# Residual rows kept in DRAM: experts' outputs added by accumulating scatters

## The chip, the cores and the metric

One core of a Trainium2 chip. The metric is the device time of one execution in microseconds (us). TensorE multiplies matrices, VectorE, ScalarE and GpSimd compute elementwise, SyncE issues transfers; all of a core's transfers run on its 16 DMA engines. SBUF is the memory on the chip, with 128 partitions, PSUM takes TensorE's results, and DRAM (HBM) is the memory outside.

## The reference

Four sublayers change x, which has 32 x 256 tokens of 128 floats:

```
x = x + attention_a(layernorm(x))       # 16 heads, product of two score matrices, causal
x = x + experts(layernorm(x))           # layer 0
x = x + attention_b(layernorm(x))       # features, softmax over 256 tokens, causal
x = x + experts(layernorm(x))           # layer 1, same weights

experts(x):
  feat   = x as 8192 rows of 128
  norm   = layer_norm(feat, g, b)
  scores = norm @ centroids.T                       # 8 experts
  for each expert in turn: the 1024 best tokens that no earlier expert took
  routed = feat[chosen tokens]                      # 8 x 1024 x 128
  h      = gelu(layer_norm(routed, g, b) @ w1 + b1) @ w2 + b2    # 128 -> 512 -> 128
  out    = routed + h, put back at the tokens' places
```

Each token is chosen by exactly one expert. The experts get a normalised x, so x + experts(layernorm(x)) is x + layernorm(x) + h: the first two terms are x times a factor plus a shift for each token, and h is the experts' own row.

## The kernel before

x stays in SBUF for the whole kernel, as `k["x"]`: 64 tiles of 128 tokens (token 128 n + p lies in partition p of tile n), 4 MB. The kernel is a row of phases, each with its own blocks for the engines. `phase` (line 74) calls the body, has GpSimd clear the phase's semaphores and then holds all engines at a barrier, so no phase overlaps the next. `build` lists them: load_x, statistics, attention_a, normalise_for_experts, experts, add_rows, statistics, attention_b, normalise_for_experts, experts, add_rows. Two DRAM tensors of 8192 rows lie between phases: `norm_rows` holds the normalised rows that the experts gather, `ffn_rows` takes the experts' outputs.

`experts` (line 798) works in turns (`plan`, line 913): in turn e the engines search the tokens of expert e (VectorE compares, TensorE counts), list those of expert e - 1 as row numbers, and compute expert e - 2. What each engine does in it:

- SyncE (lines 937 to 956) loads the weights of expert e, and from expert 2 on waits for the copy of expert e - 2's output first (`y_copied`), since two sets of weight buffers take turns. After expert 7 it has nothing left.
- ScalarE starts with a pass over the 64 tiles of x in place (line 1263): x times a factor plus a shift, which is x + layernorm(x). Each tile raises `x_done`. Then it copies and activates for the experts; line 1296 copies an expert's output from PSUM into the buffer `yb`, in two halves, and waits until the scatters of the expert two before have left that buffer.
- GpSimd gathers (line 1321) and scatters (line 1328): eight indirect DMAs each for an expert, each of 128 rows of 512 bytes, with the row numbers from the list `index`. In turn e it scatters expert e - 3, half by half, and then gathers expert e - 1; in the last turn it scatters expert 7 too. All of these go through GpSimd's own DMA queue. At the end it waits until all scatters have landed (line 1346).
- TensorE turns the gathered rows (line 1150), multiplies with w1 (line 1159) and w2 (line 1169).

The scatters of before write h alone into `ffn_rows`. `add_rows` (line 1349) then reads `ffn_rows` back in the order of the tokens, in eight groups of eight tiles (0.5 MB) through four buffers, and VectorE adds each group to x (line 1382). For layer 0 VectorE then measures mean and variance of the group's eight tiles (`bn_stats`, line 1386), which the next statistics phase needs. For layer 1 ScalarE stores each group to the output instead (line 1374).

The functions that the change touches:

Of the kernel before, what the change touches and what calls it, by code (L numbers as in the profile page):

```python
# [13 lines left out]
F32 = mybir.dt.float32  # L14
# [4 lines left out]
ALU = mybir.AluOpType  # L19
# [3 lines left out]
P = 128  # L23
D = 128
B, T = 32, 256
TOKENS = B * T
TILES = TOKENS // P
# [23 lines left out]
def wait_apart(eng, semaphore, value, passed):  # L51


    eng.wait_ge(semaphore, value)
    eng.sem_inc(passed, 1)
# [14 lines left out]
def phase(nc, body, *args):  # L70

    used = []

    def sem(name):
        used.append(nc.alloc_semaphore(name))
        return used[-1]

    body(nc, sem, *args)
    nc.clear_and_free_semaphores(used)
    nc.all_engine_barrier()  # L80


def build(nc, d):
    with ExitStack() as whole:
        def keep(name, shape, dt=F32):
            return whole.enter_context(nc.sbuf_tensor(name, shape, dt))

        k = {
            "x": keep("x", [P, TILES, D]),
            "ident": keep("ident", [P, P]),  # L90
            "rstd": keep("rstd", [P, TILES]),
            "shift": keep("shift", [P, TILES]),
            "halves": keep("halves", [P, TILES, 6]),
            "high_key": keep("high_key", [P, E, TILES], U16),
            "low_key": keep("low_key", [P, E, TILES], U16),
            "rstd_1": keep("rstd_1", [P, TILES]),
            "gain": keep("gain", [P, 1]),
            "bias": keep("bias", [P, 1]),
            "cent": keep("cent", [P, 32]),
            "digits": keep("digits", [P, PASSES, CANDS], U32),  # L100
            "weight": keep("weight", [P, PASSES]),
            "before": keep("before", [P, P], BF16),
            "lanes": keep("lanes", [P, P, TILES // CHUNKS], BF16),
            "place": keep("place", [P, 2 * SLOTS, TILES], BF16),
            "eighth": keep("eighth", [P, 2 * SLOTS, TILES], BF16),
            "w_all": keep("kept_w_all", [P, FEAT + D]),
            "w_shell": keep("kept_w_shell", [SHELL, D]),
            "omega_t": keep("kept_omega_t", [SHELL, RFF]),
            "b_shell": keep("kept_b_shell", [SHELL, P]),
            "b_all": keep("kept_b_all", [P, FEAT + D]),  # L110
            "b_rff": keep("kept_b_rff", [P, RFF]),
            "temp": keep("kept_temp", [P, 1]),
            "decay": keep("kept_decay", [P, T]),
            "c_mag": keep("kept_c_mag", [P, NM]),
            "w_comb": keep("kept_w_comb", [P, 3, P]),
            "w_out": keep("kept_w_out", [P, D]),
            "b_out": keep("kept_b_out", [P, D]),
            "bar": keep("kept_bar", [P, P], BF16),
            "ident_b": keep("kept_ident_b", [P, P], BF16),
            "b_consts": nc.alloc_semaphore("attention_b_consts"),  # L120
            "consts": nc.alloc_semaphore("expert_consts"),
            "norm_consts": nc.alloc_semaphore("norm_consts"),
        }
        k["scores"] = keep("scores", [P, E, TILES])
        norm_rows = nc.dram_tensor("norm_rows", (TOKENS, D), F32, kind="Internal").ap()
        ffn_rows = nc.dram_tensor("ffn_rows", (TOKENS, D), F32, kind="Internal").ap()
        phase(nc, load_x, d, k)
        phase(nc, statistics, k, "a")
        phase(nc, attention_a, d, k)
        phase(nc, normalise_for_experts, d, k, norm_rows, 0)  # L130
        phase(nc, experts, d, k, norm_rows, ffn_rows, 0)
        phase(nc, add_rows, k, ffn_rows, None, 0)
        phase(nc, statistics, k, "b")
        phase(nc, attention_b, d, k)
        phase(nc, normalise_for_experts, d, k, norm_rows, 1)
        phase(nc, experts, d, k, norm_rows, ffn_rows, 1)
        phase(nc, add_rows, k, ffn_rows, d["out"], 1)
        nc.clear_and_free_semaphores([k["consts"], k["norm_consts"], k["b_consts"]])
        nc.all_engine_barrier()

# [657 lines left out]
def experts(nc, sem, d, k, norm_rows, ffn_rows, layer):  # L798
# [4 lines left out]
    tag = f"e{layer}"  # L803
    per = TILES // CHUNKS
# [4 lines left out]
    with ExitStack() as ctx:  # L809
# [60 lines left out]
        rows = [sb(f"rows{i}", [P, SLOTS, D]) for i in range(2)]  # L870
# [3 lines left out]
        yb = [sb(f"yb{i}", [P, SLOTS, D]) for i in range(2)]  # L874
# [34 lines left out]
        y_copied = sem(f"y_copied_{tag}")  # L909
        scattered = [sem(f"scattered{i}_{tag}") for i in range(2)]  # L910
        wait_passed = sem(f"passed_{tag}")

        def plan(eng, turn):

# [22 lines left out]
        with nc.Block() as block:  # L937
            @block.sync
            def _(sp):
                def turn(e, par, half):  # L940
                    if isinstance(e, int) and e >= E:
                        return
                    at = bass.ds(e, 1) if not isinstance(e, int) else slice(e, e + 1)
                    w1_src = d["L0_ffn_w1"][at, :, :].rearrange("a p f -> (a p) f")
                    w2_src = d["L0_ffn_w2"][at, :, :].rearrange("a (p c) n -> (a p) c n", c=FC)
                    b1_src = d["L0_ffn_b1"][at, :].rearrange("a (p c) -> (a p) c", c=FC)
                    b2_src = d["L0_ffn_b2"][at, :].broadcast_to([P, D])

                    if not isinstance(e, int) or e > 1:
                        sp.wait_ge(y_copied, 2 * e - 2)  # L950
                    sp.dma_start(w1[par][:], w1_src).then_inc(wl[par], 16)
                    sp.dma_start(w2[par][:], w2_src).then_inc(wl[par], 16)
                    sp.dma_start(b1[par][:], b1_src).then_inc(wl[par], 16)
                    sp.dma_start(b2[par][:], b2_src).then_inc(wl[par], 16)

                plan(sp, turn)

# [354 lines left out]
            def _(pool):  # L1312
# [10 lines left out]

                def scatter(c, par, half, h):
                    part = slice(h * SLOTS // 2, (h + 1) * SLOTS // 2)
                    wait_apart(pool, y_copied, 2 * c + h + 1, wait_passed)
                    for j in range(part.start, part.stop):
                        pool.indirect_dma_start(ffn_rows, bass.IndirectOffsetOnAxis(ap=list_of(c, par)[:, j:j + 1], axis=0),  # L1328
                                                yb[par][:, j, :], None).then_inc(scattered[par], 16)

                def turn(e, par, half):
                    _, lists, compute = does(e)
# [13 lines left out]
                    pool.wait_ge(scattered[par], 16 * SLOTS * (E // 2))  # L1346


def add_rows(nc, sem, k, rows_dram, out, layer):

    tag = f"r{layer}"
    steps = 8
    per = TILES // steps
    with ExitStack() as ctx:
        buf = [ctx.enter_context(nc.sbuf_tensor(f"buf{i}_{tag}", [P, per, D], F32)) for i in range(4)]
        loaded = [sem(f"rows_loaded{i}_{tag}") for i in range(4)]
        added = sem(f"rows_added_{tag}")
        measured = sem(f"rows_measured_{tag}")
        stored = sem(f"out_stored_{tag}")
        rows = rows_dram.rearrange("(n p) d -> p n d", p=P)  # L1360
        out_v = out.rearrange("b (t p) d -> p (b t) d", p=P) if out is not None else None
        with nc.Block() as block:
            @block.sync
            def _(sp):
                for g in range(steps):
                    if g >= 4:
                        sp.wait_ge(added, g - 3)
                    sp.dma_start(buf[g % 4][:], rows[:, g * per:(g + 1) * per, :]).then_inc(loaded[g % 4], 16)  # L1368
            if out is not None:
                @block.scalar  # L1370
                def _(act):
                    for g in range(steps):
                        act.wait_ge(added, g + 1)
                        act.dma_start(out_v[:, g * per:(g + 1) * per, :], k["x"][:, g * per:(g + 1) * per, :]).then_inc(stored, 16)
                    act.wait_ge(stored, 16 * steps)

            @block.vector
            def _(dve):
                for g in range(steps):
                    dve.wait_ge(loaded[g % 4], 16 * (g // 4) + 16)  # L1380
                    part = k["x"][:, g * per:(g + 1) * per, :]
                    dve.tensor_tensor(part, part, buf[g % 4][:], ALU.add).then_inc(added, 1)  # L1382
                    if out is None:
                        dve.wait_ge(added, g + 1)
                        for n in range(g * per, (g + 1) * per):
                            dve.bn_stats(k["halves"][:, n, :], k["x"][:, n, :]).then_inc(measured, 1)


def attention_b(nc, sem, d, k):
# [567 lines left out]
```

## Time and profile before

| | us |
|---|---|
| median of 3 runs (lowest to highest) | 1505.43 (1504.72 to 1506.91) |
| profiled execution, its own time | 1510.9 |
| its span, first to last instruction | 1509.1 |
| experts, layer 0, from SyncE's first load to GpSimd's last scatter | 591.2 to 891.5 |
| add_rows, layer 0, from the first reload to the last statistics | 896.5 to 923.0 |
| experts, layer 1, end of the last scatter | 1475.2 |
| add_rows, layer 1, from the first reload to the span's end | 1480.3 to 1509.1 |

A line of the timeline gives the start from the span's beginning, the duration, the engine, the line of the kernel, the operation with its output and inputs, how many instructions are merged in it, and in brackets how long the engine had stood idle and what ended that. PE is TensorE, PEld its weight load, DVE VectorE, ACT ScalarE, POOL GpSimd, SP SyncE; SPq is SyncE issuing DMAs, and its duration is that of the issuing, not of the transfer.

### The profile page before, as it was taken

How to read it: one execution, taken by the hardware profiler on the slowest of the kernel's cores; microseconds unless marked ns; L12 is line 12 of the kernel's file. 1: busy time of each engine (PE TensorE's matmuls, PEld its weight loads, DVE VectorE, ACT ScalarE, POOL GpSimd, SP SyncE). 2: the span in 40 equal slices, each digit the busy share in tenths (PEclk: the TensorE clock that was granted, in tenths of full speed). 3: DMA queues.
4: the chain of work that ended last, by engine and by line, in shares of the span. 5: the costliest groups of instructions: out<-in, count | busy, mean ns of one | idle time of the engine just before them, and what ended most of it. 6: DMA issues, size and time to landing. Idle time of an engine off the chain costs nothing. (4 is left out here: it accounts for less than half of the span.)

```text
span 1509.1 us, 33959 instructions
## 1 busy us (share of the span) xinstructions
PE 1156.4 (77%) x11356; PEld 742.7 (49%) x11356; DVE 921.9 (61%) x2822; ACT 701.2 (46%) x1485; POOL 731.0 (48%) x712
## 2 busy tenths in 40 slices
PE   0799999999999966478887942769996358888790
PEld 0244444444444433156655732659993136666570
DVE  4477767777777757887764016845557786766102
ACT  0477676767767637322222314655554602322240
POOL 0478878787878840045456430045550024545540
PEclk9999999999999987579998875979998559999895
DMA  6000000000000004011121132000003101111118
GB/s 167 4 2 0 0 0 0 0 0 0 0 0 0 1 6 140 2 28 50 45 67 55 50 85 53 0 1 0 0 0 112 33 15 46 50 52 49 56 50 229
DMA packets 67979, 54.64 MB, mean 36 GB/s; under 512 B 12864, under 2 KB 57280, under 8 KB 67904
## 3 DMA queue, kind: packets, MB, share of 16 engines
q1 hardware_dynamic: 51392, 32.70, 7.8%
q0 software_dynamic: 8192, 16.79, 3.8%
q10 hardware_dynamic: 8320, 4.19, 0.9%
q8 instruction: 42, 0.69, 0.2%
q14 instruction: 33, 0.27, 0.1%
HBM read 32.69 MB, written 20.97 MB: 36 GB/s over the span
## 5 line engine op out<-in xcount | busy, mean ns | idle before, releaser
L353 POOL TENSOR_TENSOR patt_aa<-patt_aa,causal_aa 128x512 f32<-128x512 f32 x256 | 319.4, 1273 | 73.6 <-DVE patt_aa L477 71.8
L477 DVE TENSOR_TENSOR patt_aa<-p_second_aa,first_aa 128x512 f32<-128x512 f32 x384 | 247.5, 686 | 136.2 <-ACT first_aa L410 132.5
L410 ACT ACTIVATE first_aa<-p_first_aa 128x512 f32<-128x512 f32 x384 | 208.7, 597 | 139.0 <-PE p_first_aa L568 135.1
L1321 POOL DMA_INDIRECT rows_e<-norm_rows,index_e x128 | 123.8, 967 | 269.5 <-DVE index_e L1037 210.2
L568 PE MATMUL p_second_aa<-q_t_aa,k_t_aa 32*128 32x512 f32 x768 | 235.4, 642 | 0.0
L568 PE MATMUL p_first_aa<-q_t_aa,k_t_aa 32*128 32x512 f32 x768 | 217.4, 642 | 15.7 <-ACT first_aa L410 15.4
L1328 POOL DMA_INDIRECT ffn_rows<-yb_e,index_e x128 | 128.1, 1001 | 163.5 <-ACT yb_e L1296 129.9
L1237 PE MATMUL p_cnt_e<-reach_e,ones_e 128*128 128x240 bf16 x448 | 88.0, 330 | 82.4 <-DVE reach_e L1083 76.6
L1159 PE MATMUL p_h_e<-rows_t_e,w_e 128*128 128x512 f32 x256 | 146.1, 694 | 0.2
L1288 ACT ACTIVATE hid_e<-p_h_e,b_e 128x512 f32<-128x512 f32 x128 | 88.0, 687 | 125.1 <-PE p_h_e L1159 102.9
L587 PEld LDWEIGHTS p_z_aa<-patt_aa,v_aa 128*32 128x32 f32 x3072 | 72.4, 109 | 147.5 <-issue 78.9
L1169 PE MATMUL p_y_e<-w_e,hid_e 128*128 128x128 f32 x1024 | 144.1, 286 | 0.3 <-issue 0.2
L1169 PEld LDWEIGHTS p_y_e<-w_e,hid_e 128*128 128x128 f32 x1024 | 133.0, 203 | 0.8 <-issue 0.6
L587 PE MATMUL p_z_aa<-patt_aa,v_aa 128*32 128x128 f32 x3072 | 124.1, 279 | 2.8 <-POOL patt_aa L353 2.8
L568 PEld LDWEIGHTS p_first_aa<-q_t_aa,k_t_aa 32*128 32x128 f32 x768 | 57.7, 183 | 97.9 <-ACT first_aa L410 88.7
L1382 DVE TENSOR_TENSOR x<-x,buf_r 128x1024 f32<-128x1024 f32 x16 | 19.5, 1218 | 141.1 <-DMA buf_r<-ffn_rows 141.1
L1278 ACT ACTIVATE rows_t_e<-p_t_e,bias,gain 128x512 f32<-128x512 f32 x32 | 25.0, 781 | 171.9 <-PE p_t_e L1150 171.9
L347 POOL TENSOR_TENSOR roped_aa<-straight_aa,crossed_aa 128x512 f32<-128x512 f32 x64 | 81.3, 1271 | 44.7 <-DVE crossed_aa L467 44.7
L1237 PEld LDWEIGHTS p_cnt_e<-reach_e,ones_e 128*128 128x128 bf16 x448 | 39.8, 110 | 128.1 <-DVE reach_e L1083 94.3
L1159 PEld LDWEIGHTS p_h_e<-rows_t_e,w_e 128*128 128x128 f32 x256 | 71.5, 317 | 36.5 <-issue 33.0
L397 ACT ACTIVATE q_t_aa<-p_turn_aa,own_aa 128x512 f32<-128x512 f32 x128 | 81.6, 698 | 2.5 <-PE p_turn_aa L551 2.5
L1096 DVE TENSOR_REDUCE count_e<-p_cnt_e 128x15 f32<-128x240 f32 x112 | 45.4, 406 | 52.3 <-PE p_cnt_e L1237 28.5
(242 smaller groups left out, 2158.2 us busy)
## 6 DMA issues: line engine op xcount, KB each, us to landing
norm_rows<-norm_n SPq DMA_DIRECT2D x32, 256.0 KB, 2.4
w_e<-L_ffn_w SPq DMA_DIRECT2D x32, 256.0 KB
buf_r<-ffn_rows SPq DMA_DIRECT2D x16, 512.0 KB, 6.2
out<-x ACTq DMA_DIRECT2D x8, 512.0 KB, 8.5
rows_e<-norm_rows,index_e POOLq DMA_INDIRECT x128
ffn_rows<-yb_e,index_e POOLq DMA_INDIRECT x128
b_e<-L_ffn_b SPq DMA_DIRECT2D x16, 64.0 KB
lanes<-c_lanes SPq DMA_DIRECT2D x1, 256.0 KB, 2.8
```

Source lines behind the costliest of these rows:

```text
L353: pool.tensor_tensor(patt[n % LAG][:, b, :, :], patt[n % LAG][:, b, :, :], causal[:, None, :].broadcast_to([P, 4, P]), ALU.mult).then_inc( ...
L397: act.activation(q_t[par][:, :, j, :], p_turn[:, :].rearrange("p (h q) -> p h q", h=HALVES), ACT.Identity, scale=own[:, j:j + 1]).then_inc ...
L410: act.activation(first[n % 2][:, b, :], p_first[b][:], ACT.Identity).then_inc(first_copied, 1)
L477: dve.tensor_tensor(patt[n % LAG][:, b, :, :].rearrange("p h q -> p (h q)"), p_second[(2 * n + b) % ROOMS][:], first[n % 2][:, b, :], ALU. ...
L568: pe.matmul(out[:], k_t[par][rows, half, keys * P:(keys + 1) * P], q_t[par][rows, half, :, queries * P:(queries + 1) * P], start=True, sto ...
L587: mm = pe.matmul(p_z[32 * c:32 * c + 32, queries * P:(queries + 1) * P], v[par][:, keys, 32 * h:32 * h + 32], patt[n % LAG][:, b, c, :], s ...
L1159: pe.matmul(p_h[m % 2][:], w1[par][:, f:F:FC], rows_t[:, h * 512:(h + 1) * 512], start=True, stop=True).then_inc(up_done, 1)
L1169: mm = pe.matmul(p_y[t // 4][:, (t % 4) * D:(t % 4 + 1) * D], hid[:, f, t * P:(t + 1) * P], w2[par][:, f, :], start=False, stop=(f == FC - 1))
L1237: mm = pe.matmul(p_cnt[:, 0:SPAN * CANDS], ones[:], reach[:, q // 2, :, (q % 2) * SPAN:(q % 2 + 1) * SPAN], start=(q == 0), stop=(q == TIL ...
L1288: act.activation(hid[:, f, h * 512:(h + 1) * 512], p_h[m % 2][:], ACT.Gelu_apprx_tanh, bias=b1[par][:, f:f + 1]).then_inc(gelu_done, 1)
L1321: pool.indirect_dma_start(rows[lpar][:, j, :], None, norm_rows, bass.IndirectOffsetOnAxis(ap=list_of(l, lpar)[:, j:j + 1], axis=0)).then_i ...
L1328: pool.indirect_dma_start(ffn_rows, bass.IndirectOffsetOnAxis(ap=list_of(c, par)[:, j:j + 1], axis=0), yb[par][:, j, :], None).then_inc(sc ...
```

## The change

The experts' phase now also stores x to DRAM. After the weights of expert 1 SyncE issues eight stores of eight tiles each, each as soon as ScalarE has finished those tiles; they go to the tensor that the experts' rows are scattered into. The scatters add to what lies there (`compute_op=ALU.add`) instead of overwriting it, and the first of them waits until all eight stores have landed. For layer 1 that tensor is the kernel's output itself, and nothing follows. For layer 0 it is `ffn_rows`, and the phase behind loads it straight over x in eight loads without buffers, with the statistics of each group and without an add.

```
-        phase(nc, add_rows, k, ffn_rows, None, 0)
+        phase(nc, load_rows, k, ffn_rows)
...
-        phase(nc, experts, d, k, norm_rows, ffn_rows, 1)
-        phase(nc, add_rows, k, ffn_rows, d["out"], 1)
+        phase(nc, experts, d, k, norm_rows, d["out"].rearrange("b t d -> (b t) d"), 1)
...
+        x_stored = sem(f"x_stored_{tag}")
+        parts = 8
...
+                def store_x():
+                    for q in range(parts):
+                        tiles = slice(q * TILES // parts, (q + 1) * TILES // parts)
+                        sp.wait_ge(x_done, (q + 1) * TILES // parts)
+                        sp.dma_start(ffn_rows.rearrange("(n p) d -> p n d", p=P)[:, tiles, :], k["x"][:, tiles, :]).then_inc(x_stored, 16)
...
                     sp.dma_start(b2[par][:], b2_src).then_inc(wl[par], 16)
+                    if e == 1:
+                        store_x()
...
                 def scatter(c, par, half, h):
                     part = slice(h * SLOTS // 2, (h + 1) * SLOTS // 2)
+                    if c == 0 and h == 0:
+                        pool.wait_ge(x_stored, 16 * parts)
                     wait_apart(pool, y_copied, 2 * c + h + 1, wait_passed)
                     for j in range(part.start, part.stop):
                         pool.indirect_dma_start(ffn_rows, bass.IndirectOffsetOnAxis(ap=list_of(c, par)[:, j:j + 1], axis=0),
-                                                yb[par][:, j, :], None).then_inc(scattered[par], 16)
+                                                yb[par][:, j, :], None,
+                                                compute_op=ALU.add).then_inc(scattered[par], 16)
...
+def load_rows(nc, sem, k, rows_dram):
+
     steps = 8
     per = TILES // steps
...
+    loaded = [sem(f"rows_loaded{g}") for g in range(steps)]
+    measured = sem("rows_measured")
+    rows = rows_dram.rearrange("(n p) d -> p n d", p=P)
+    with nc.Block() as block:
+        @block.sync
+        def _(sp):
+            for g in range(steps):
+                sp.dma_start(k["x"][:, g * per:(g + 1) * per, :], rows[:, g * per:(g + 1) * per, :]).then_inc(loaded[g], 16)
+
+        @block.vector
+        def _(dve):
+            for g in range(steps):
+                dve.wait_ge(loaded[g], 16)
+                for n in range(g * per, (g + 1) * per):
+                    dve.bn_stats(k["halves"][:, n, :], k["x"][:, n, :]).then_inc(measured, 1)
```

## Rows read from the trace of the kernel before

**Rows 1.** The page: the span, and its 40 slices of TensorE.
```profile
span 1509.1 us, 33959 instructions
...
PE   0799999999999966478887942769996358888790
```

**Rows 2.** The chain that ended last: by line, and its last piece.
```profile
by line: DMA buf_r<-ffn_rows 1.2%; DVE x L1382 0.2%; SPq L1368 0.1%; issue 0.0%
...
1501.40 1.23 DVE x L1382
```

**Rows 3.** Timeline of the span's end, layer 1's last scatters and reload.
```profile
1465.37 0.96 POOL L1328 DMA_INDIRECT ffn_rows<-yb_e,index_e  x1 [6.50 <-ACT yb_e L1296]
...
1474.27 0.97 POOL L1328 DMA_INDIRECT ffn_rows<-yb_e,index_e  x1 [0.30 <-issue]
1480.28 12.23 SPq L1368 DMA_DIRECT2D buf_r<-ffn_rows  x8
1484.51 1.23 DVE L1382 TENSOR_TENSOR x<-x,buf_r 128x1024 f32<-128x1024 f32 x1 [66.49 <-DMA buf_r<-ffn_rows]
```

**Rows 4.** By stretch: PE, PEld, DVE, ACT, POOL busy, clock, DMA share, GB/s.
```profile
1492.00:1496.00 4.00, 0.00 (x0) 0.00 (x0) 1.89 (x2) 0.00 (x0) 0.00 (x0) 0.50 1.15 347
```

**Rows 5.** Timeline of add_rows after layer 0, and the next phase's first instruction.
```profile
896.51 14.00 SPq L1368 DMA_DIRECT2D buf_r<-ffn_rows  x8
900.49 1.23 DVE L1382 TENSOR_TENSOR x<-x,buf_r 128x1024 f32<-128x1024 f32 x1 [66.35 <-DMA buf_r<-ffn_rows]
901.75 1.64 DVE L1386 BATCH_NORM_STATS2 halves<-x 128x6 f32<-128x128 f32 x8
...
921.36 1.64 DVE L1386 BATCH_NORM_STATS2 halves<-x 128x6 f32<-128x128 f32 x8
923.78 0.06 DVE L212 MEMSET eps_b<- 128x1 f32 x1 [0.78 <-PEq L80]
```

**Rows 6.** GpSimd's DMA queue, 640 to 892: packets, MB, share of 16 engines.
```profile
q0 software_dynamic: 4064, 8.33, 11.3%
```

**Rows 7.** By stretch: the reload of layer 0, and the features behind it.
```profile
898.00:900.00 2.00, 0.00 (x0) 0.00 (x0) 0.00 (x0) 0.00 (x0) 0.00 (x0) 0.50 0.98 290
...
908.00:910.00 2.00, 0.00 (x0) 0.00 (x0) 2.00 (x7) 0.00 (x0) 0.00 (x0) 0.50 0.92 243
...
936.00:950.00 14.00, 13.59 (x77) 12.47 (x75) 9.64 (x28) 13.87 (x35) 0.00 (x0) 0.94 0.00 0
```

**Rows 8.** ScalarE's pass over x (timeline); SyncE's waits: total, times, longest.
```profile
591.24 24.73 ACT L1263 ACTIVATE x<-x,shift,rstd 128x128 f32<-128x128 f32 x64 [4.18 <-PEq L80]
...
SPq L951 <- ACT yb_e L1296: 213.1, 5, 93.4
```

**Rows 9.** Scatters' and gathers' lines; queue and 40 slices, 1465 to 1476.5; a 16 KB load.
```profile
L1328 POOL DMA_INDIRECT ffn_rows<-yb_e,index_e x128: 963/969/1435, 677.0 to 1474.3; - x128
...
L1321 POOL DMA_INDIRECT rows_e<-norm_rows,index_e x128: 940/944/1170, 638.5 to 1427.5; - x128
...
DMA  0000005100060006000140006000320006000510
...
q0 software_dynamic: 256, 0.52, 13.4%
...
rope_aa<-c_rope SPq DMA_DIRECT2D x1, 16.0 KB, 2.0
```

**Rows 10.** Timeline: gathers, TensorE's turning of their rows, a scatter.
```profile
704.78 0.94 POOL L1321 DMA_INDIRECT rows_e<-norm_rows,index_e  x1 [0.30 <-issue]
...
715.54 0.60 PE L1150 MATMUL p_t_e<-ident,rows_e 128*128 128x128 f32 x4
...
1413.73 0.94 POOL L1321 DMA_INDIRECT rows_e<-norm_rows,index_e  x1 [0.30 <-issue]
...
1431.17 1.00 POOL L1328 DMA_INDIRECT ffn_rows<-yb_e,index_e  x1 [2.69 <-ACT yb_e L1296]
1431.31 0.60 PE L1150 MATMUL p_t_e<-ident,rows_e 128*128 128x128 f32 x4
```

More of the change, by code:

```diff
@@ L1346, in _ @@
                     pool.wait_ge(scattered[par], 16 * SLOTS * (E // 2))
-def add_rows(nc, sem, k, rows_dram, out, layer):
-    tag = f"r{layer}"
+def load_rows(nc, sem, k, rows_dram):
     steps = 8
     per = TILES // steps
[L1354 to L1386, printed above, removed]
```

## The prediction

> **What bounds the kernel now.** I read the page first, then the chain that ended last, then the timeline around both places where the experts' stage hands over, then the scatters and gathers inside it.
>
> The page's slices show TensorE at 9 tenths for much of the span of 1509.1 us, but at nothing in the last slice of 37.7 us [rows 1], and the chain of waits is nothing but the last stage: 1.2% of the span in the reload, 0.2% in the adds, down to the add at 1501.40 [rows 2]. So the kernel is a row of stages, and two of them are pure data movement in which TensorE stands still. The second one: GpSimd's last scatter ends at 1475.24, SyncE's first reload is issued at 1480.28, VectorE's first add starts at 1484.51, and the span ends at 1509.1 [rows 2, 3]. The reader is to see that eight adds of 1.23 us are spread over 18 us: they wait for loads, and from 1492 the loads share the engines with the output's stores at 347 GB/s in total [rows 4]. The first one, after layer 0, has the same head (first reload 896.51, first add 900.49), but here VectorE is the bound: one add of 1.23 us and eight statistics of 1.64 us together for each of eight groups, without a gap that a load causes, until 923.00 [rows 5].
>
> Inside layer 0's experts' stage GpSimd's queue, with 64 gathers and 64 scatters per layer, takes 11.3% of 16 engines [rows 6]: transfers are not what its turns wait for. At the stage's end the last matmuls, the last copy and the last scatters follow each other.
>
> **The change part by part.** All sums are first against the profiled execution: span 1509.1, its own time 1510.9, so 1.8 us lie around the span. The median shown is 1505.43, 5.5 us below that execution. I carry the difference over unchanged.
>
> 1. Last stage dropped. The span's part from the first reload to the end is 1509.1 - 1480.28 = 28.8 us [rows 1, 3]. What remains is the final clearing of three semaphores and one barrier. A hand-over between two phases costs VectorE 0.78 us from its last instruction to its next [rows 5], with a block's end in it, so the rest is between 0 and 0.78; I take 0.4. Gain 28.4 us. The 5.04 us between the last scatter's end and 1480.28 (landing, GpSimd's block end, barrier) stay.
>
> 2. Layer 0's stage becomes a plain load. No buffer is waited for, so the loads run at their own rate. The trace shows 290 GB/s from 898 to 900, where four groups are on the way [rows 7]: 0.524 MB / 0.29 = 1.81 us a group. First group ready at 900.49 as now, the eighth at 900.49 + 7 x 1.81 = 913.2, its eight statistics 1.64: 914.8. The first seven groups' statistics (1.64 each) hide under the loads by 0.17 us each. Before: 923.0. Gain 8.2 us. Bounds: 9.8 us if loads were no limit (8 adds of 1.23); 5 us if they ran at 243 GB/s, as in 908 to 910 (2.16 a group, end 917.3, gain 5.7). What is late next is the load, not VectorE.
>
> 3. x stored from SyncE: eight DMAs of 0.5 MB per layer, behind the weights of experts 0 and 1. ScalarE writes the 64 tiles from 591.24 to 615.97 [rows 8], so a part of eight tiles is ready every 3.1 us, and a store of 0.524 MB needs 1.5 us at the 347 GB/s of the mixed stretch or 1.8 at 290. Landed by about 619. The first scatter, which now waits for it, is issued at 677.0 [rows 9]: 58 us of cover. SyncE's next work is the weights of expert 2, which wait for the copy of expert 0's output: its longest wait in the stage is 93.4 us, and the stores fall into it [rows 8]. The first gather comes at 638.5 [rows 9], 19 us behind the last store. Cost 0; without the cover 14.5 us (4.19 MB at 290) per layer. Nothing behind GpSimd's new wait is late: the wait is passed before its first scatter's own condition is met.
>
> 4. Accumulating scatters. The trace has none, so two prices are open.
>    GpSimd's issue: a plain scatter takes 0.97 us and 0.30 between two, a pitch of 1.27; the gather's median is 0.94 [rows 3, 9]. Eight follow each other at each stage's end (1465.37 to 1475.24), and none of them waits for its input behind the first (8.90 us from the first start to the last are seven pitches) [rows 3]. So the pitches of eight lie on the path, to first order. Lower end: the gather's 0.94, -0.2 us per layer. Upper end: twice the issue, 0.97 more each, +7.8 us. I take 0.1 more each, near the scatter's own row since the list and the rows are the same: +0.8 per layer.
>    The drain: eight scatters took 13.4% of 16 engines in 11.5 us, 0.19 us of each engine per scatter, in bursts that fill at most two slices of 0.29 us [rows 9]. An engine moves eight rows for each scatter. If the destination must be read as well, twice the work is 0.39 us, under the pitch of 1.27, and only the last one's own end is later. (The trace has no accumulating DMA to check that against.) Lower end 0. Upper end, as long as rows overlap: one more round trip, for which the nearest row is a 16 KB DMA's 2.0 us from issue to landing [rows 9]. I take 1.0 per layer. If rows don't overlap it is a rival (below).
>    Both layers: 2 x (0.8 + 1.0) = 3.6 us.
>
> 5. Do the other users of GpSimd's queue suffer? Gathers stand behind scatters. In the middle of the stage the last gather behind expert 0's scatters ends at 705.72, and TensorE turns those rows at 715.54: 9.8 us of slack, less about 1 for the landing. At layer 1's end expert 6's last gather ends at 1414.67 and its rows are turned at 1431.31, 16.6 us later [rows 10]. So with four scatters just ahead nothing on TensorE moves up to about 2.2 us a scatter in the queue (4 x 2.2 = 8.8).
>
> Sum: -28.4 - 8.2 + 3.6 = -33.0. Own time 1510.9 - 33.0 = 1477.9; against the median 1505.43 - 33.0 = 1472.4.
>
> TensorE's clock: it is granted 0.50 in both stretches that shrink, since the engine does nothing, and 0.94 from 936 to 950 as soon as it works [rows 7]. I expect the same rise 8 us earlier and no gain or loss.
>
> **The rivals.**
> A. GpSimd's issue doubles, because it has to describe the read of the destination beside the source and the write. For: it is software that runs per row, 0.97 us for 128 rows. Against: gather and scatter differ by only 3%. Price: 2 x 7.8 for the issue and 2 x 1.0 for the drain instead of 3.6, so -36.6 + 17.6 = -19.0: 1486.4.
>
> B. The queue drains too slowly, and the change ends slower. Mechanism: each row becomes a read, an add and a write of its own, and takes as long as a whole burst takes now, 0.4 us (between one and two slices of 0.29) [rows 9]. Place: the last 24 scatters of a layer. In layer 1 the first of them is generated by 1432.17 [rows 10], and the last has landed by 1476.2, the end of the last busy slice [rows 9]; VectorE has nothing left there, so the queue's backlog is the stage's end. At 8 x 0.4 = 3.2 us a scatter: 1432.2 + 24 x 3.2 = 1509.0, 32.8 late per layer, against 36.6 / 2 = 18.3 gained per layer: +29.0, 1534.4. Since the stretch has idle gaps, nothing is lost up to (1476.2 - 1432.2) / 24 = 1.83 us a scatter, and the change turns slower from (1476.2 + 18.3 - 1432.2) / 24 = 2.6 us on, 13 times the engine time of now. For it: a read and a dependent write per row. Against: today's bursts show eight rows moved in 0.19 us, so that rows overlap. In the extreme, with every row waiting out 2.0 us alone, a scatter is 16 us, 64 are 1024 us, and the kernel is about twice as long; that is the far end of the unknown cost and I leave it out of the range.
>    The Trainium skill bears on this in "DMA: Bandwidth & Descriptors", section "Two DMAs through the same engine are not ordered": of two read-modify-write packets of one row on one queue, the second mostly read stale data when it directly followed, and never with five or more between. Read as five in flight over 2.0 us, this is 0.4 us a row, an estimate that gives B's time; read as proof of overlap it speaks for the forecast. No row here tells which.
>
> C. The drain lies between: 1.83 to 2.6 us a scatter. At 2.2, 1432.2 + 24 x 2.2 = 1485.0, 8.8 late per layer: -36.6 + 1.6 + 17.6 = -17.4, 1488.0.
>
> D. The cover of the store fails or the load is slower than its row: at most 14.5 x 2 and 2.5. The first would need a first scatter 58 us earlier; I give it nothing.
>
> **How the numbers follow.** Forecast (parts 1 to 5) 0.68; A 0.13; C 0.06; B 0.12, the extreme in it 0.02; a time within 0.2% of before (about 3 us, what a measurement of this kernel can tell from no change; it needs a drain near 2.55) 0.01. Faster is the forecast, A and C: 0.87. The forecast's own range: all gained at the lower ends of part 4, with 9.8 in part 2 and 28.8 in part 1, is -39.0 (1466); +2.0 for the upper drain of 2.0 per layer and +2.5 for slow loads on top of 1472.4 give 1477. The range reaches to A and C: 1466 to 1491, and leaves out B and a part of A.
>
> **What would show it.** The timeline's end: right if nothing but barriers follows GpSimd's last scatter by about 6 us; wrong if more than 10 us lie there (drain, B or C). GpSimd's row of the scatters: mean 1.0 to 1.1 us and pitch under 1.5 (forecast), near 1.9 (A). Layer 0's hand-over: VectorE without adds, gaps between groups of eight statistics, about 14.3 us from the first to the last. SyncE's eight stores between 594 and 617 and no engine waiting for them. The queue's row for GpSimd: its share of 16 engines over the experts' stage, 11.3% now [rows 6], about 16% by the forecast (64 x 0.2 us more in 252) and over 80% with B. TensorE's turns at the same distances. The prediction is wrong if an accumulating scatter costs over 1.83 us in the queue or over 1.6 us in GpSimd's issue.

## The result and the profile after

| | before | changed |
|---|---|---|
| median, lowest to highest, us | 1505.95 (1504.72 to 1506.91), 4 runs | 1482.94 (1478.40 to 1487.19), 4 runs |
| ratio of the times, 95% interval | | 0.9837 [0.981, 0.9864] |
| profiled execution: own time, span | 1510.9, 1509.1 | 1487.19, 1485.4 |
| TensorE's mean granted clock | 0.886 | 0.892 |

The runs of before are the three shown ahead and one more. The change gains 23.0 us by the medians, 23.7 by the two profiled executions. The forecast was 33.0.

The page of the changed kernel, with the lines that answer to [rows 1] (PE is TensorE's busy share and PEclk its granted clock in tenths, in 40 slices of 37.1 us): the nearly idle last slice is gone.
```profile
span 1485.4 us, 33918 instructions
...
PE   0799999999999975468888680849996647888864
...
PEclk9999999999999997569999795869998757999977
```

GpSimd's timeline at the end of layer 1, which answers to [rows 3]. Nothing but landing, block end and barriers follows the last line: it ends at 1478.12, the span at 1485.4.
```profile
1463.51 1.56 POOL L1339 DMA_INDIRECT out<-yb_e,index_e  x1 [3.29 <-ACT yb_e L1305]
1465.38 1.56 POOL L1339 DMA_INDIRECT out<-yb_e,index_e  x1 [0.31 <-issue]
...
1474.70 1.56 POOL L1339 DMA_INDIRECT out<-yb_e,index_e  x1 [0.30 <-issue]
1476.56 1.56 POOL L1339 DMA_INDIRECT out<-yb_e,index_e  x1 [0.30 <-issue]
```
The issue of a scatter takes 1.56 us where it took 0.97, and the next one starts 1.86 us after it instead of 1.27. The eight now take 14.6 us from the first start to the last end, where they took 9.9.

The same around layer 0's hand-over, to be read against [rows 5]: the last scatter, the loads' issues, VectorE's statistics, and the next phase's first instruction.
```profile
894.56 1.55 POOL L1339 DMA_INDIRECT ffn_rows<-yb_e,index_e  x1 [0.31 <-issue]
902.98 11.79 SPq L1372 DMA_DIRECT2D x<-ffn_rows  x8
907.06 1.65 DVE L1379 BATCH_NORM_STATS2 halves<-x 128x6 f32<-128x128 f32 x8 [89.35 <-DMA x<-ffn_rows]
908.86 1.65 DVE L1379 BATCH_NORM_STATS2 halves<-x 128x6 f32<-128x128 f32 x8 [0.16 <-DMA x<-ffn_rows]
...
914.32 1.65 DVE L1379 BATCH_NORM_STATS2 halves<-x 128x6 f32<-128x128 f32 x8 [0.20 <-DMA x<-ffn_rows]
916.81 5.00 DVE L1379 BATCH_NORM_STATS2 halves<-x 128x6 f32<-128x128 f32 x24 [0.85 <-DMA x<-ffn_rows]
922.61 0.06 DVE L211 MEMSET eps_b<- 128x1 f32 x1 [0.80 <-PEq L80]
```
The adds are gone and each of the next four groups of statistics waits 0.16 to 0.20 us for its load, as the forecast had it; the sixth waits 0.85, the last two do not wait. But the first load is issued at 902.98, and it was at 896.51 before.

The durations of layer 0's scatters and of all gathers (min/median/max ns; of before in [rows 9]):
```profile
L1339 POOL DMA_INDIRECT ffn_rows<-yb_e,index_e x64: 1552/1553/1747, 677.0 to 894.6; - x64
...
L1330 POOL DMA_INDIRECT rows_e<-norm_rows,index_e x128: 940/947/1360, 638.5 to 1419.2; - x128
```
GpSimd's DMA queue from 640 to 892 (packets, MB, share of 16 engines; before in [rows 6]), and behind it the queue of SyncE from 590 to 640, where x is stored:
```profile
q0 software_dynamic: 10832, 8.20, 24.9%
...
q1 hardware_dynamic: 9472, 5.38, 36.8%
```
The same bytes go in more than twice the packets and twice the engine time, yet the queue stays three quarters empty.

Where the 23.7 us come from, from one clearing of the semaphores to the next (in the records of GpSimd's instructions):

| us | before | changed | difference |
|---|---|---|---|
| experts, layer 0 | 305.2 | 311.6 | +6.4 |
| add_rows / load_rows | 27.3 | 19.7 | -7.6 |
| attention_b and what lies around it | | | +1.1 |
| experts, layer 1 | 305.6 | 310.5 | +4.8 |
| from there to the end | 29.3 | 0.9 | -28.4 |

The two experts' stages hide more than their differences show. Up to layer 0's expert 5 the changed kernel's turns are shorter (most are 30.7 us against 31.8, from one expert's first gather to the next's), and then it loses the lead: from expert 5's first scatter to expert 7's it takes 43.0 us (838.6 to 881.6) where the kernel before takes 34.3 (847.3 to 881.6), and 43.1 against 34.2 in layer 1. In that time TensorE, which otherwise starts eight products of this kind in 1.1 us, starts one in 0.7 us for some 15 us, with nothing that the profile shows to wait for:
```profile
830.79 0.37 PE L1178 MATMUL p_y_e<-w_e,hid_e 128*128 128x128 f32 x1 [0.94 <-issue]
831.50 0.27 PE L1178 MATMUL p_y_e<-w_e,hid_e 128*128 128x128 f32 x1 [0.33 <-issue]
832.21 0.37 PE L1178 MATMUL p_y_e<-w_e,hid_e 128*128 128x128 f32 x1 [0.45 <-issue]
```
The same stands at 1411 to 1427 in layer 1, and in none of the other traces of this document. What causes it is not known.

### The profile page after: what moved, and what is told of

It is laid out like the page before. It is cut to its first block and busy times, and to the rows that moved or that the text cites. A ratio compares the mean times of both kernels' runs of the same rounds, so it can differ in the third digit from the quotient of the medians.

```text
span 1485.4 us, 33918 instructions
## 1 busy us (share of the span) xinstructions
PE 1157.9 (78%) x11356; PEld 745.3 (50%) x11356; DVE 901.1 (61%) x2806; ACT 701.1 (47%) x1485; POOL 809.1 (54%) x712
## 3 DMA queue, kind: packets, MB, share of 16 engines
q0 software_dynamic: 22528, 16.79, 8.7%
HBM read 28.49 MB, written 25.17 MB: 36 GB/s over the span
## 5 line engine op out<-in xcount | busy, mean ns | idle before, releaser
L1330 POOL DMA_INDIRECT rows_e<-norm_rows,index_e x128 | 127.3, 994 | 247.0 <-DVE index_e L1046 209.2
L1178 PE MATMUL p_y_e<-w_e,hid_e 128*128 128x128 f32 x1024 | 148.4, 287 | 12.7 <-issue 12.4
L1168 PE MATMUL p_h_e<-rows_t_e,w_e 128*128 128x512 f32 x256 | 139.4, 662 | 0.1
L1339 POOL DMA_INDIRECT ffn_rows<-yb_e,index_e x64 | 101.0, 1578 | 58.6 <-ACT yb_e L1305 38.9
L1339 POOL DMA_INDIRECT out<-yb_e,index_e x64 | 101.8, 1591 | 56.8 <-ACT yb_e L1305 38.4
L1305 ACT ACTIVATE yb_e<-p_y_e 128x512 f32<-128x512 f32 x32 | 19.1, 598 | 144.7 <-remote 88.4
L1168 PEld LDWEIGHTS p_h_e<-rows_t_e,w_e 128*128 128x128 f32 x256 | 71.1, 316 | 32.4 <-issue 27.4
```

Source lines behind the costliest of these rows:

```text
L1168: pe.matmul(p_h[m % 2][:], w1[par][:, f:F:FC], rows_t[:, h * 512:(h + 1) * 512], start=True, stop=True).then_inc(up_done, 1)
L1178: mm = pe.matmul(p_y[t // 4][:, (t % 4) * D:(t % 4 + 1) * D], hid[:, f, t * P:(t + 1) * P], w2[par][:, f, :], start=False, stop=(f == FC - 1))
L1330: pool.indirect_dma_start(rows[lpar][:, j, :], None, norm_rows, bass.IndirectOffsetOnAxis(ap=list_of(l, lpar)[:, j:j + 1], axis=0)).then_i ...
```

## The experiments

The chips that served fall into two kinds. On two of them the kernel before takes 1438 to 1439 us, on the first and on one more 1506 to 1508; what differs is told at the end. Every ratio below is against the kernel before on the same chip. The changed kernel itself ran on the first chip and on one of the 1438 kind only, so where another version is compared with it across chips, the ratios are compared.

### The adding alone taken away

x is stored and waited for, but the scatters overwrite; the output lacks the part of x.
```diff
-                                                yb[par][:, j, :], None,
-                                                compute_op=ALU.add).then_inc(scattered[par], 16)
+                                                yb[par][:, j, :], None).then_inc(scattered[par], 16)
```


> The changed kernel with its scatters overwriting instead of adding: x + layernorm(x) is missing from the output and from what layer 1 reads; everything else, the stores of x included, as in the changed kernel. Theory (the accumulating scatter costs GpSimd 1.55 us instead of 0.97, lands 0.5 us later and lengthens GpSimd's drain by 1.3 us, 6.5 us at each stage's end): the scatters are back at 0.97 us, the drain at 2.7, and the time is 11 to 13 us below the changed kernel, near 1471, 0.977 of before. Rival (the stores of x or the changed order in the stage cost the time): it stays within 3 us of the changed kernel's 1483, ratio 0.983 to 0.985.

Measured: 1402.82 us beside 1437.9, ratio 0.9754 [0.9739, 0.9769]. That is 35.1 less than before, and parts 1 and 2 of the prediction make 36.6, as measured above 36.0. So all but about 1 us of what the change gives back is the price of adding in the scatter. The ratio is the expected one, but the expectation's price was not: the changed kernel takes 1427.35 on the other chip of this kind (below), 24.5 more than this version, and not 11 to 13.

### The store alone added

The kernel before, with x stored to a tensor that nobody reads, and the first scatter waiting for it.
```diff
+                        sp.dma_start(k["x_spare"].rearrange("(n p) d -> p n d", p=P)[:, tiles, :], k["x"][:, tiles, :]).then_inc(x_stored, 16)
...
+                    if c == 0 and h == 0:
+                        pool.wait_ge(x_stored, 16 * parts)
```


> The kernel before, with x also stored in the experts' stages to a DRAM tensor that nobody reads, and the first scatter waiting for it. Theory (the store is covered): within 1.5 us of before, ratio 0.999 to 1.001. Rival (the store disturbs the stage by its transfers): 5 us or more slower, ratio above 1.003.

Measured: 1438.81 beside 1437.9, ratio 1.0006 [0.9997, 1.0015]. The store is free to within 2 us for both layers.

### The change in one layer only

`experts` gets a flag for the store, the wait and the adding; the other layer stays as before.
```diff
-def experts(nc, sem, d, k, norm_rows, ffn_rows, layer):
+def experts(nc, sem, d, k, norm_rows, ffn_rows, layer, onto=True):
...
+                                                **({"compute_op": ALU.add} if onto else {})).then_inc(scattered[par], 16)
```
In layer 0 only:

> The change in layer 0 alone; layer 1 is that of before. Theory: 7.6 us gained in the load and 6.5 lost at the stage's end, so 1 us faster at most, ratio 0.998 to 1.001. Rival (the layers share the gain as predicted, 8.2 less 1.8 in layer 0): 6.4 us faster, ratio 0.996.

In layer 1 only:

> The change in layer 1 alone; layer 0 is that of before. Theory: 28.4 us gained at the end and 6.5 lost at the stage's end, 22 us faster, about 1484, ratio 0.985 to 0.987: the whole gain of the change comes from here. Rival (prediction's sizes, 28.4 less 1.8): 26.6 us faster, ratio 0.982.

Measured: layer 0 alone 1441.81, ratio 1.0029 [1.0018, 1.0039]; layer 1 alone 1422.9, ratio 0.9899 [0.9884, 0.9914]. The changed stage is 281.2 us in the one and 281.3 in the other, the unchanged one beside it 269.6 in the first. Both lie outside what was expected (0.998 to 1.001, and 0.985 to 0.987), which took 6.5 us a layer. On this chip adding costs a layer 12 us, not the 1.8 of the forecast: layer 0 loses more than its 7.6, and all the net gain is layer 1's dropped stage.

### Both kernels again, traced on a chip of the 1438 kind

> The kernel before, for its trace on the same chip: if its experts' stage is near 269 us, TensorE's granted clock shows no dips between 657 and 850; if near 305, it shows several of 3 us to the lower level.

> The changed kernel once more, beside the kernel before on the same chip. The runs of parts of the change were on a chip on which the kernel before took 1437.9 us and TensorE's clock had no dips in the experts' stage; there accumulating scatters lengthened the stage by 12.4 us per layer. Theory (without dips GpSimd's last 24 scatters at 1.86 us each are the stage's end, with dips they partly hide in TensorE's slower turns): on a chip without dips the ratio is the product of the two layers alone, 1.0029 x 0.9899 = 0.993, on one with dips near 0.984. Rival (the cost of an accumulating scatter is fixed at 6.5 us a layer): 0.984 on any chip.

Measured: the kernel before 1437.36 in its traced run and 1438.81 in the nine beside it, the changed one 1427.35, ratio 0.992 [0.9906, 0.9933]. The product of the two single layers is 1.0029 x 0.9899 = 0.9928: they add up, as the expectation's theory had it, and a price that is the same on any chip (0.984) is refuted. The experts' stages are 268.8 and 269.6 us before, 280.7 and 282.5 changed.

The kernel before, GpSimd's timeline from the first scatter of expert 5 to the last of expert 7, layer 0:
```profile
815.20 1.00 POOL L1328 DMA_INDIRECT ffn_rows<-yb_e,index_e  x1 [0.30 <-issue]
...
835.06 0.97 POOL L1328 DMA_INDIRECT ffn_rows<-yb_e,index_e  x1 [0.30 <-issue]
842.52 0.97 POOL L1328 DMA_INDIRECT ffn_rows<-yb_e,index_e  x1 [6.49 <-ACT yb_e L1296]
...
851.42 0.97 POOL L1328 DMA_INDIRECT ffn_rows<-yb_e,index_e  x1 [0.30 <-issue]
```
The changed kernel, the same stretch:
```profile
817.96 0.94 POOL L1330 DMA_INDIRECT rows_e<-norm_rows,index_e  x1 [0.30 <-issue]
819.21 1.62 POOL L1339 DMA_INDIRECT ffn_rows<-yb_e,index_e  x1 [0.30 <-issue]
...
849.05 1.55 POOL L1339 DMA_INDIRECT ffn_rows<-yb_e,index_e  x1 [0.30 <-issue]
...
862.06 1.55 POOL L1339 DMA_INDIRECT ffn_rows<-yb_e,index_e  x1 [0.30 <-issue]
```
Look at the brackets. Before, GpSimd stands idle for 6.49 us ahead of expert 7's first scatter, because it waits for ScalarE's copy, and so for TensorE. In the changed kernel there is no such wait: 24 scatters follow each other in 24 x 1.86 = 44.6 us, and expert 7's rows lie ready while GpSimd still issues expert 6's. The engine that the prediction treated as waiting has become the bound for the last three experts. The start of expert 7's scatters moves from 842.5 to 849.05, +6.5 (1.0 of it was there when the stage began). Then come 8 x 0.59 = 4.7 for its own eight, and 1.8 until the next phase: 12.0 without the 1.0, as the stages say.

### The last expert's scatters overwrite

Expert 7's rows, an eighth of the output, lack x.
```diff
+                                                **({"compute_op": ALU.add} if c < E - 1 else {})).then_inc(scattered[par], 16)
```


> The changed kernel with expert 7's scatters overwriting: x + layernorm(x) is missing for that expert's tokens. Theory: the last eight pitches fall from 1.86 to 1.27 (4.7 us per layer), landing by 0.5 and the drain by up to 1.3 if the drain goes by the last scatters' kind: 9.5 to 13 us below the changed kernel of this call, 0.7 to 0.9%. Rival (a drain that goes by all accumulating scatters of the phase): 10 to 10.5 us, with the drain still near 4 us in the trace. Rival (only the queue's length counts and the last expert is nothing special): under 3 us.

Measured on the chip of the pair above: 1415.55, ratio 0.9838 [0.9825, 0.9851], 11.8 us below the changed kernel, 5.9 a layer: 4.7 for the eight issues, 0.4 for the last one's landing (1.53 us from its end to the drain against 1.97), and 0.8 that no record explains. GpSimd's drain at the block's end, 3.97 us in the changed kernel and 2.67 in the kernel before (in the records of its instructions), is still 3.97 here. So the drain does not go by the last scatters. With the whole cost at 24.8 us for two layers (stages), 13.0 are left for the other seven experts and the drain: 2 x 1.3 for the drain and, by subtraction, 10.4 for the queue in front of GpSimd.

### Only the last expert's scatters add

All rows but expert 7's lack x.
```diff
+                                                **({"compute_op": ALU.add} if c == E - 1 else {})).then_inc(scattered[par], 16)
```


> The changed kernel with only expert 7's scatters adding: x + layernorm(x) is missing for all other tokens. Theory (an adding scatter costs 0.59 us of issue; GpSimd is free when expert 7's rows are ready): 8 x 0.59 + 0.5 + 1.3 = 6.5 us per layer more than with overwriting scatters alone (0.9754 of before), so 0.984 to 0.985, and the changed kernel's further 6 us per layer come from the queue of experts 5 to 7. Rival (the price lies in the landing in DRAM of whatever is queued): as the changed kernel, 0.992.

Measured on a chip of the 1507 kind: 1481.43 beside 1507.68, ratio 0.9827 [0.9811, 0.9843]. The changed kernel has 0.9837 [0.981, 0.9864] on the first chip, of the same kind. The intervals cover each other, so on this kind the adding in the 56 other scatters of a layer has no price clear of noise, where it was 6.5 us a layer above. Part of the reason stands in the trace, GpSimd's first scatters of experts 6 and 7 here:
```profile
858.78 0.97 POOL L1339 DMA_INDIRECT ffn_rows<-yb_e,index_e  x1 [6.11 <-ACT yb_e L1305]
...
876.69 1.61 POOL L1339 DMA_INDIRECT ffn_rows<-yb_e,index_e  x1 [6.51 <-ACT yb_e L1305]
```
TensorE's turns are longer on this kind, 17.9 us lie between the two, and even eight pitches of 1.86 (14.9) fit in. The changed kernel waits for ScalarE in the same place (the 3.29 above, and 3.35 in layer 0), so GpSimd's queue is not the bound of its last turn there.

That the other 56 cost nothing is not shown by this. The turns here are 31.8 to 32.8 us and expert 7's first scatter comes 33.9 us after expert 5's, where the changed kernel has 30.7 and 43.0: the two differ by more than the adding, and the differences cancel. And one part of the price is missing here. The drain is 2.67 us, the value of the kernel before, although eight scatters of each layer add. It was expected to grow by 1.3. So the drain grows with the adding scatters of experts 0 to 6 and not with those of expert 7. The changed kernel with all its scatters overwriting was not run on this kind, so the split by parts is less firm than on the other.

### The sum made before the scatter, in SBUF

If adding in the scatter is dear and the dropped stage is the gain, x can come with the gather. Each row of `norm_rows` gets 1 KB, the normalised row and x beside it; SyncE stores x there, the gathers fetch both, and the sum is made before an overwriting scatter: by GpSimd for experts 0 to 4 and by VectorE for 5 to 7.
```diff
+        norm_rows = nc.dram_tensor("norm_rows", (TOKENS, 2 * D), F32, kind="Internal").ap()
...
+        rows = [sb(f"rows{i}", [P, SLOTS, 2 * D]) for i in range(3)]
...
+                        dve.tensor_tensor(yb[c % 2][:, 4 * h:4 * h + 4, :], p_y[h][:, :].rearrange("p (t n) -> p t n", n=D),
+                                          rows[c % 3][:, 4 * h:4 * h + 4, D:2 * D], ALU.add).then_inc(y_copied, 1)
```


> A version that keeps the dropped last stage and accumulates nothing: SyncE stores x into the second half of norm_rows' rows (now 1 KB), the gathers fetch both halves in one DMA, GpSimd adds x to the experts' rows for experts 0 to 4 and VectorE, idle by then, for 5 to 7 in place of ScalarE's copy; the scatters overwrite. Three row buffers. Theory (an accumulating scatter's price is GpSimd's 0.59 us each and the longer landing and drain): stages back at their length before, so 0.975 to 0.978 of the kernel before, faster than both. Rival (gathers of 1 KB rows and GpSimd's two additions of 1.3 us per expert put as much back): 0.985 or more.

Measured: 1413.8 (1412.49 to 1415.62) beside 1438.81, ratio 0.9829 [0.9815, 0.9842], 13.5 us below the changed kernel on the same chip: the fastest whole version there. Gathers of 1 KB rows cost GpSimd no more issue than those of 512 bytes, and its scatters are cheap again:
```profile
L1336 POOL DMA_INDIRECT rows_e<-norm_rows,index_e x128 | 124.9, 976 | 247.4 <-DVE index_e L1047 209.6 <-issue 37.8
...
L1346 POOL DMA_INDIRECT ffn_rows<-yb_e,index_e x64 | 63.6, 993 | 26.3 <-issue 16.1 <-DVE yb_e L1145 7.4 <-POOL yb_e L1343 2.8
```
(Columns: total and mean duration, idle time before and what ended it.) The stages are 273.8 and 275.0, so 5 us a layer are still lost, and the ratio lies between the theory (0.975 to 0.978) and the rival (0.985 or more). The turns are 28.1 to 29.6 us where they were 27.3. Whether GpSimd's adds or the wider gathers lengthen them was not separated.

The same with TensorE adding x through a multiplication by the identity, into the sum that it forms anyway:
```diff
+                        pe.matmul(p_y[t // 4][:, (t % 4) * D:(t % 4 + 1) * D], k["ident"][:], rows[c % 3][:, t, D:2 * D], start=False, stop=False)
```


> The version with 1 KB rows once more, but TensorE adds x: one more matmul per tile with the identity into the same sum, eight per expert of about 0.13 us each; GpSimd adds nothing and ScalarE copies for all experts again. Theory (the version before lost 0.8 us per turn of 27.3 to GpSimd's additions): turns of 27.3 to 27.8 us, 0.976 to 0.980 of the kernel before. Rival (TensorE is the turn's bound, and 1.1 us more on it is a turn longer by as much; or the 1 KB gathers cost it): turns of 28.1 or more, 0.983.

Measured on the chip of the 1507 kind: 1489.41, ratio 0.987 [0.9851, 0.9889]. The theory (0.976 to 0.980) is missed. It beats before; against the changed kernel's 0.9837 [0.981, 0.9864] on the first chip it is not clear of noise. A likely reason is that each tile's addition lies on TensorE's path: it takes 0.22 us there, not the expected 0.13, and so 1.8 us a turn. But the version with GpSimd's adds was not run on this kind, so the additions' price is not shown apart from that of the wider gathers.

And the last expert's output copied and scattered in four pieces instead of two:
```diff
+                        for q in range(4):
+                            act.wait_ge(two_down, q + 1)
```


> The same, and expert 7's output copied in four pieces from four banks instead of two, so that its first scatter starts about 2.2 us earlier. Theory (GpSimd's eight pitches of 1.27 us behind the first piece are the stage's end): 2.0 to 2.2 us less per layer, 4 in all, ratio 0.003 below the kernel with TensorE's additions. Rival (the last piece's copy sets the end): under 2 us in all.

Measured: 1485.38, ratio 0.985 [0.9835, 0.9866], 4.0 us below the version without the quarters, as expected. In layer 0 expert 7's first scatter starts at 882.8 instead of 886.0 (0.75 of it was there when the stage began).

## Why the prediction was right in its place and wrong in a size

The sign was right, and so was the mechanism of the gain: a stage dropped, a plain load, a store that costs nothing. 1482.94 lies in the range of 1466 to 1491, but above the forecast's own range (up to 1477) and nearer to rival A's 1486.4 than to the forecast's 1472.4. The range was hit because it reached to the rivals, and in part by luck: on the chip of the 1438 kind the change gains 11.5 us, a third of the forecast. In the profiled executions on the first chip the terms of the sum come out so:

1. Last stage dropped, -28.4: measured -28.4. Six microseconds were to follow the last scatter, 7.3 do.
2. Plain load, -8.2: measured -7.6. The first five groups came 1.80 to 1.84 us apart, as the term has it, the sixth was late by 0.85.
3. The store, 0: 0 (1.0006 [0.9997, 1.0015] alone). The stores stand in SyncE's timeline from 594.99 on:
```profile
594.99 21.43 SPq L945 DMA_DIRECT2D ffn_rows<-x  x8
```
4. Accumulating scatters. **This is the step that failed: "I take 0.1 more each, near the scatter's own row since the list and the rows are the same: +0.8 per layer."** The issue costs 0.59 more, 4.7 a layer. The argument was that gather and scatter cost the same, so that the kind of transfer does not matter. For adding it does. Rival A put the rise at +0.97; the measured one is 60% of that, and the mark set for A (a pitch near 1.9) is what the timeline shows. Whether A's reason, a description of the destination's read, is the true one is not shown. What the records do show is that an adding scatter goes as 128 packets of one row of 512 bytes, where an overwriting one goes as 16 packets of eight rows. The drain, taken as 1.0 a layer, was 1.8: 0.5 from the last scatter's own landing and 1.3 from GpSimd's drain. On the first chip the terms with their measured sizes make -28.4 - 7.6 + 9.4 + 3.6 = -23.0, for 23.7 measured. That they agree so well is luck too. The 6.5 a layer (4.7 + 0.5 + 1.3) is what lies behind expert 7's first scatter, and that scatter starts at 881.6 in layer 0 before and after only because turns that are shorter and last turns that are 9 us longer, told above, cancel. In layer 1 they leave 1.7 in favour of the change, and attention_b takes 1.1 more.
5. Gathers not delayed: they were not (638.5 in both, expert 2's at 695.8 and 696.6). But the question was too narrow. Step 5 asked who waits behind scatters up to 2.2 us in the queue of transfers; it did not ask whether 24 issues in a row still fit beside TensorE's last three turns. "The pitches of eight lie on the path, to first order" holds on the first chip, where GpSimd still waits 3.35 us ahead of expert 7, and fails on chips with shorter turns, where the queue in front of GpSimd costs another 5 us a layer.

Rivals B and C are refuted. In the records of the DMA engines the burst of one of the last scatters lasts 0.74 to 0.90 us where it lasted 0.33 to 0.34; that is far under 1.83 or 2.6, and 24.9% is the queue's share where B needed over 80%. B took a row at 0.4 us, the length of a whole burst before. The estimate that the prediction drew from the Trainium skill, "DMA: Bandwidth & Descriptors", section "Two DMAs through the same engine are not ordered", came to the same figure, with its five packets read as five in flight over 2.0 us. The measured burst, about 0.1 us a row and engine, speaks against that reading: the rows of one scatter overlap or follow closely.

What stays open: where the 0.59 us of the issue go; why GpSimd's drain grows by 1.3 us when the scatters of experts 0 to 6 add, and not when only expert 7's do; why TensorE slows down for 15 us in the changed kernel on the first chip; and why the changed kernel's runs spread over 9 us on the first chip and over 1.4 on the other kind.

## What to carry to other kernels

Price a DMA that adds at its destination by the issue first: here 1.56 us of GpSimd for 128 rows instead of 0.97, while the DMA engines had room for twice the work. Such an issue is not "on the path for the last eight" only; multiply it by the work of the last few turns and see whether the issuing engine's idle brackets still hold it. A stage in which all engines but one stand still is worth dropping even at that price, but look for a way that pays it elsewhere: fetching the summand with the gather took rows of 1 KB and no more of GpSimd's issue, and lost 5 us a layer in place of 12.

## What was not expected of the hardware

- The issue of an adding scatter: 1.55 us against 0.97, on every chip used. Gathers are unchanged at 0.947 median.
- An adding scatter of 512-byte rows goes as one packet per row: 22528 packets in the queue over the run against 8192, and the queue's share of 16 engines rises from 11.3% to 24.9% (640 to 892). The pages count 28.49 MB read from HBM against 32.69; the 4.20 less are the one reload of x that is gone, so the destinations' 8.4 MB appear in no count of reads.
- GpSimd's drain at the block's end: 3.97 us in every stage in which all experts' scatters or all but the last expert's add, 2.67 where none adds or only the last expert's eight do.
- The two kinds of chips. One turn of the experts' stage (from one expert's first gather to the next's) takes 27 us on the one and about 32 on the other, while the rest agrees within some 3 us (588 and 591 us to the stage of layer 0, 280 and 278 between the two stages, 29.3 behind). TensorE's granted clock differs: the kernel before from 640 to 860 and from 1200 to 1400 (TensorE, its weight load, VectorE, ScalarE, GpSimd busy; clock; DMA share; GB/s), first chip:
```profile
640.00:860.00 220.00, 179.40 (x1340) 132.69 (x1341) 129.99 (x497) 57.27 (x83) 109.50 (x111) 0.88 0.17 51
1200.00:1400.00 200.00, 158.41 (x1236) 115.07 (x1237) 144.06 (x559) 43.65 (x63) 83.47 (x85) 0.84 0.14 41
```
and the chip of the 1438 kind:
```profile
640.00:860.00 220.00, 188.77 (x1500) 146.64 (x1498) 126.24 (x487) 66.62 (x97) 121.77 (x125) 0.94 0.19 56
1200.00:1400.00 200.00, 184.49 (x1464) 144.16 (x1461) 115.49 (x446) 66.60 (x97) 115.79 (x119) 0.98 0.19 58
```
Inside layer 0's stage the first chip falls to the lower of the two clocks in seven stretches between 657 and 849, the other in none, as was expected of that trace. That is too little for 36 us a layer: the 256 products with w1 take 694 ns in the mean on the one and 651 on the other, which is 11 us over both layers. And the slow kind is slow at the full clock too. From 657 to 820 the kernel before on the 1438 kind, and the version with TensorE's additions on the 1507 kind:
```profile
657.00:820.00 163.00, 153.06 (x1232) 118.77 (x1232) 110.30 (x427) 54.44 (x80) 97.84 (x100) 1.00 0.21 63
657.00:820.00 163.00, 140.43 (x1169) 109.42 (x1167) 111.18 (x426) 45.21 (x66) 78.30 (x80) 1.00 0.22 67
```
At a granted clock of 1.00 in both, a turn takes 27.3 us on the one and 32.4 on the other, of which the eight additions are 1.8. Most of the rest shows as waits of VectorE, once a turn each, for which the profile names a transfer that landed long ago or nothing on this core (kernel before, first chip, 657 to 820: total, times, longest):
```profile
DVE count_e L1096 <- DMA norm_rows<-norm_n: 9.2, 4, 3.2
DVE quarters_e L1027 <- remote: 5.4, 4, 1.4
```
The kernel before has neither wait on the 1438 kind. The changed kernel on the first chip has only the first of them, which fits its turns of 30.7 us instead of 31.8. What holds VectorE in them stays open.
